# The norms of query and key moved from VectorE to GpSimd in a fused attention and feed-forward kernel, with a new merge order of its streams

## The reference

```
h = layernorm(x) * (1 + ca) + sa
x = x + ga * attention_A(h)       # 16 heads of 8; softmax over 512 keys of k.v * temperature, applied to q
h = layernorm(x) * (1 + cb) + sb
x = x + gb * F(h)                 # F is two layers, below
# one layer of F, 8 heads of 64:
  q, k, v = split(shift_token(x) @ wqkv)
  q = q / clip(norm(q), 1e-12) * q_scale ;  k = the same with k_scale    # one norm per token and head
  q, k = rotary_xpos(q, k)
  x = x + local_attention(q, k, v) @ wo      # windows of 64 tokens, each sees itself and the one before
  h = layernorm(shift_token(x)) * g + b
  x = x + (a * gelu(g')) @ w2 + b2           # a, g' = split(h @ w1 + b1)
```

## Time and profile before

| | |
|---|---|
| median of 3 runs | 1196.69 us (1193.58 to 1197.32) |
| the profiled execution, whole | 1196.15 us |
| its span, first to last instruction | 1194.3 us |
| busy of the span: PE, DVE, ACT, POOL | 997.0, 949.4, 918.2, 508.1 us |
| mean granted PE clock | 0.948 of full speed |

### The profile page before, as it was taken

One profiled execution on the slowest core, in us unless ns is written; L12 is line 12 of the kernel. 1 busy time (PEld: TensorE's weight loads), 2 busy tenths in 40 slices (PEclk: granted clock), 3 DMA queues, 4 the chain that ended last, 5 costly groups with the idle time before them and its releaser, 6 DMA issues. The chain is left out here.

```text
span 1194.3 us, 23996 instructions
## 1 busy us (share of the span) xinstructions
PE 997.0 (83%) x8124; PEld 510.0 (43%) x8124; DVE 949.4 (79%) x1947; ACT 918.2 (77%) x2782; POOL 508.1 (43%) x578
## 2 busy tenths in 40 slices
PE   2677787768888798778868897899999789999898
PEld 2232232223323352234336444655664357545664
DVE  4789898888869777986884699779769976789865
ACT  1698979899978988887659566868886587958983
POOL 5012143212105321343474058647823676348830
PEclk8699989999989898998989998999999999999999
DMA  5541305232204103001011001101110020001200
GB/s 206 180 142 36 106 1 146 62 107 71 72 0 130 43 28 115 10 10 24 1 31 34 10 1 32 33 1 32 33 41 10 10 63 16 18 1 32 46 20 27
DMA packets 28009, 59.18 MB, mean 50 GB/s; under 512 B 6192, under 2 KB 6384, under 8 KB 26736
## 3 DMA queue, kind: packets, MB, share of 16 engines
q1 hardware_dynamic: 27120, 56.33, 16.7%
q10 hardware_dynamic: 768, 1.31, 0.3%
HBM read 23.98 MB, written 18.87 MB: 36 GB/s over the span
## 5 line engine op out<-in xcount | busy, mean ns | idle before, releaser
L905 ACT ACTIVATE E<-psum,neg_max 128x512 f32<-128x512 f32 x512 | 346.6, 716 | 64.2 <-DVE neg_max L1191 45.9
L1191 DVE TENSOR_REDUCE neg_max<-psum 128x2 f32<-128x1024 f32 x256 | 307.5, 1214 | 58.7 <-PE psum L465 56.7
L465 PE MATMUL psum<-v_rows,k_rows 64*128 64x512 f32 x512 | 130.3, 514 | 106.0 <-ACT E L905 79.6
L998 ACT ACTIVATE rot_work<-psum,neg 128x128 f32<-128x128 f32 x512 | 184.3, 412 | 17.9 <-DVE neg L1284 11.0
L838 POOL TENSOR_TENSOR rot_work<-rot_work,rz 128x512 f32<-128x512 f32 x128 | 133.0, 1047 | 141.0 <-DVE rz L1289 140.9
L825 POOL TENSOR_TENSOR work<-work,rot_work 128x512 f32<-128x512 f32 x96 | 121.7, 1273 | 129.6 <-DVE rot_work L1262 129.3
L465 PEld LDWEIGHTS psum<-v_rows,k_rows 64*128 64x128 f32 x512 | 52.8, 196 | 250.6 <-ACT E L905 116.1
L803 POOL TENSOR_TENSOR qz<-qT,rz 128x32 f32<-128x32 f32 x128 | 30.8, 241 | 300.7 <-DVE rz L1195 299.8
L523 PE MATMUL psum<-wqkv_sb,hs 128*128 128x512 f32 x288 | 144.0, 622 | 6.8 <-DVE hs L1248 3.8
L474 PE MATMUL psum<-E,qz 128*32 128x512 f32 x1024 | 148.2, 653 | 0.2 <-POOL qz L803 0.2
L998 ACT ACTIVATION_READ_ACCUMULATOR rot_work<-psum,neg 128x1 f32 x512 | 126.7, 252 | 0.0
(11 more groups left out here) (140 smaller groups left out, 1784.7 us busy)
## 6 DMA issues: line engine op xcount, KB each, us to landing
k_rows<-k_scr SPq DMA_DIRECT2D x128, 64.0 KB, 1.9
work<-v_al SPq DMA_DIRECT2D x16, 512.0 KB, 4.4
v_rows<-v_scr SPq DMA_DIRECT2D x124, 64.0 KB, 1.9
work<-v_al SPq DMA_DIRECT2D x16, 384.0 KB, 5.7
k_scr<-hi SPq DMA_DIRECT2D x16, 256.0 KB, 3.0
k_scr<-lo SPq DMA_DIRECT2D x16, 256.0 KB, 3.3
v_scr<-hi SPq DMA_DIRECT2D x14, 256.0 KB, 2.9
v_scr<-lo SPq DMA_DIRECT2D x14, 256.0 KB, 3.1
```

Of the source, the lines that this page charges most:

```text
L465: pe.matmul(bank, k_rows[r:r + 64, half, hh, P * j:P * (j + 1)], v_rows[r:r + 64, b % 2, hh, :], start=True, stop=True).then_inc(full, 1)
L905: act.activation(E[:, (b * NG + g) % E_RING, 2 * half + m, :], pair[:, m], ACT.Exp, bias=neg_max[:, n, m:m + 1], accum_out=z[:, n, m:m + 1 ...
L998: last = act.activation(pr[s][:, u % PR_SLOTS, w, :], bank[:, 2 * W * w:2 * W * (w + 1)], ACT.Exp, bias=neg2[s][:, u, w:w + 1], accum_out= ...
L1191: dve.tensor_reduce(neg_max[:, n, :], pair, AX.X, ALU.max, negate=True).then_inc(max_ready, 1)
```

## The change

POOL now adds the upper 32 squares of each head to the lower 32, in place (`b_half`, a 128x256 add), and DVE sums 32 columns per head in a step of its own, `b_squares`, that waits for `sq_half`. The clamp, on POOL, is one `tensor_scalar` with two constants, and the `clamp` tensor and its fill go. The Newton step is on POOL in four dependent operations of 128x32; DVE's two steps of it, `b_norm` and `b_rnorm`, go. ACT's part is as it was. On POOL the order for each tile is `b_half`, then `b_rotary`; the norm of keys stands after the fourth tile, its Newton step after the fifth. `ORDER` and `BANKS` are new throughout; the steps per batch of F rise from 48 to 72 on POOL and from 87 to 95 on DVE, and stay 94 on PE and 88 on ACT.

```diff
+            def b_norm(s, k, l, w):
+                passed(pool, ss_ready[s], (k * L + l) * 2 * J + J * (2 - w))
+                v = ss[s][:, :, w, :]
+                pool.tensor_scalar(v, v, NORM_MIN2, SHIFT2, ALU.max, ALU.mult).then_inc(ss_all[s], 1)
+
+            def b_rnorm(s, k, l, w):
+                n = (k * L + l) * 2 + 1 - w
+                pool.wait_ge(ss_rsqrt[s], n + 1)
+                v, r, t = (a[s][:, :, w, :] for a in (ss, rn, nt))
+                pool.tensor_tensor(t, v, r, ALU.mult).then_inc(rn_chain[s], 1)
+                pool.wait_ge(rn_chain[s], 4 * n + 1)
+                pool.tensor_tensor(t, t, r, ALU.mult).then_inc(rn_chain[s], 1)
+                pool.wait_ge(rn_chain[s], 4 * n + 2)
+                pool.tensor_scalar(t, t, -0.5, 1.5, ALU.mult, ALU.add).then_inc(rn_chain[s], 1)
+                pool.wait_ge(rn_chain[s], 4 * n + 3)
+                pool.tensor_tensor(r, r, t, ALU.mult).then_inc(rn_chain[s], 1)
+
+            def b_half(s, k, l, n):
+                pool.wait_ge(sq_ready[s], (k * L + l) * 2 * J + n + 1)
+                v = sq[s][:, n % 2, :].rearrange("p (h a r) -> p h a r", h=H, a=2)
+                pool.tensor_tensor(v[:, :, 0], v[:, :, 0], v[:, :, 1], ALU.add).then_inc(sq_half[s], 1)
...
-                dve.tensor_reduce(ss[s][:, i, w, :], sq[s][:, n % 2, :].rearrange("p (h d) -> p h d", h=H),
+
+            def b_squares(s, k, l, n):
+                i, w = ROTATIONS[n]
+                dve.wait_ge(sq_half[s], (k * L + l) * 2 * J + n + 1)
+                dve.tensor_reduce(ss[s][:, i, w, :], sq[s][:, n % 2, :].rearrange("p (h d) -> p h d", h=H)[:, :, 0:32],
                                   AX.X, ALU.add).then_inc(ss_ready[s], 1)
-
-            def b_norm(s, k, l, w):
-                passed(dve, ss_ready[s], (k * L + l) * 2 * J + J * (2 - w))
-                v = ss[s][:, :, w, :]
-                dve.scalar_tensor_tensor(v, v, NORM_MIN2, clamp[:], ALU.max, ALU.mult).then_inc(ss_all[s], 1)
-
-            def b_rnorm(s, k, l, w):
-                dve.wait_ge(ss_rsqrt[s], (k * L + l) * 2 + 2 - w)
-                newton(ss[s][:, :, w, :], rn[s][:, :, w, :], nt[s][:, :, w, :], b_link_of(s, k)).then_inc(rn_ready[s], 1)
```

On PE, the `x` work done when the scores of A's batches 1 to 7 begin, and at A's end, is 0.0, 0.01, 0.22, 0.24, 0.39, 0.67, 1.0, 1.35 batches before and 0.0, 0.4, 0.76, 1.12, 1.37, 1.67, 2.1, 2.24 after. Before, the first `z` stands 109 letters behind the last `a` on PE, after 7 behind it; of PE's last 60 letters 31 are `z` after and 13 before. The first lines of POOL's string are:

```diff
-        "aaaaaaaaaaaaaaaaaaaaaaaaaaaaaaaaaaaaaaxaxaxaxxxaxxaxxxaaxaaaxxaxxaaaaaaaaaaaaaaaaaaaaaaaaaxxaxaaaaaa"
...
+        "aaaaaaaaaaaaaaaaaaaaaaxxxxxxxxxxxxxxxxxxxxxaaxxaxaxxxxaaaaxaxxxaxxxaxaaaaaaaaxxxxxaxxxaxxxaxaaxxxaxa"
```

More of the change, by code:

```diff
@@ new lines @@
+        "aaaaaaaaaaaaaaaaaaaaaaaaaaaaaaaaaaaaaaaaaaaaaaaaaaaaaaaaaaaaaaaxaxxxxxxxxxxaaaaaxxaaaxxxxaaaaaaaaaax"
+        "xaxxaaaaxxaaxxaxaxxxxaxaxxaaaxxxaaaaxaaaxaaaaaxaaaaxaxxxxxxaxaaaaxxxxxaaaxxxaaxaxaaaaaaaaaaxxaaxxaxa"
+        "axaaaaaaaxaaxxxaxaaaxxaaaxaaaxxxaaaaaxxxxaxaaxaxxaaaxaxaaaaaaaxaaaaaaxaaxxxxaaxaxxaaaxaaaaaaxaaaaaxx"
+        "xxxaxaxxaaxxaaaaaaaaaxxaaaaaaxxaaxxaaaaaaaaaaaaaaaaxxxxaaaxxaaxaaxaaaaaaxxxaaxxaxxxaaaxxaaxaaaxaaaax"
+        "aaaaaaaxaaaaaaaxaxxxaaxxaxaaxaaaaxaxxxxxxxxxaaaaaaaaaxaxxxxaxaaaaaaaaaxaxxxaaxxaaxaxxxxaaaxxxxaxaaax"
@@ new lines @@
+        "xaxaaxaxaaaaxaaaaaaaaxxxaxaxxaaaxxaaaaxaaaaaaaxaaxxxxxxaaaxxaaaxxaaaaaaxaaxaxxxxaaaaaaaaaaaaaaaxxxxa"
+        "aaaaaaaaaaaaaaaaaaaaaxaxaxxxxxyzxxxxzyyyyyyyyyyzzzzzzzzzxxxxxxzzxzzzyyzxxyyyyxxxxxxyxyxyyxyyzxxxzxyy"
+        "xzxzyyyzxyyyyzzyyyzyzzyzyzzzyzxxzxxxxyzzyyzyyyyzyzyyzyyyyyyyxxxxzyxzzzzzzyyxxyyyyzxxxzxxzxzzzxxxzzzz"
+        "zyyxxxyyxyxyzzxyyyzzyyzxyzyxxxxyyyxxxyyzxzzyzyzzyxzzzzyxxzxxzxxxxxxyzyyyyyzzzxxyyxxyzzxxzzzyxxxxzyyx"
+        "xyyyyyyyyxxxzxzxxzzzzxxyyzyxyyxyzxxxzxxyyyyzxyyzzzzxzzzzzxzxxyyxxxyyxyyyzzzzzzyyyxxxxxyyxyxyxxyzxzyz"
@@ new lines @@
+        "xyyxyyyyyzxyyxyyzzyxxyyzyyzyzzyyzzzxyzzzxxyyzzxyzzzyzxxxzxyyyzyyzzyzyyyyzyyyyxxyyxxzyzzyxxxxyyzzyxxx"
+        "xxzxzxzzxxxzxxzzyzxzyzyzyxxyyyzxyzyyxyyyzzyyzxyyyxxyxyxxzyxzzzzyzzyzxzyzxxzzzxxyxxxxxzzxxyyzzxzyzxyx"
+        "yxxzyzyzzyxzyxxzxxyyxxxyyyyxxyyxxxyyzzxyxyzxxxyyxzyxzzxzxxyxzyyxyyyyzzyzzzzzzzxzxzyxyzxxyyyyyzzzyzyy"
+        "xxyxyxxxxyxxyyyzxxzzyzzzzxxzzzxzzzxxyyyzzyyzzzzyyyzyyzyyyyzyzyzxxzyxyxxyxxxyyzzzzzxxxxxzzzyzzzzzzyyz"
+        "zyyxxxxyyzyxxzxyyzzxzxxyyxyyyxzyyyzzyzxxxzzzxzzzxzzzzyzzzyzzyyzyzyzzzyyzyyyzzzzz"
@@ L104 @@
[L104 to L108, removed]
+        "aaaaaaaaaaaaaaaaaaaaaaaaaaaaaaaaaaaaaaaaaaaaaxxaxaaxxxxxxxxxxxaaaaxxaxaxxaxxaaaaxxaxxaaaxxaxxxxaxxax"
@@ L122 @@
 BANKS = (
[L123 to L133, removed]
+    "0123424024024023502350135023550224602640240240240240264603606360631436023501502350245604624024045246"
+    "1014603046301350130135013501045630013506236032501634016351356154302460240245140204254025035012402246"
+    "0520461201460264023403252014526056406240245024651236056360131351345150123501305244204626410520420626"
+    "4024062325302513051340624023502350260246406134530506240652605406131402450143125350245012305204454202"
+    "4540134036145403013061351300451203156024602402646012603105351024130501345602402402402345024024024024"
+    "0240201073435743257326376723242324276733707605047466707327067007601270276405127523262040261242616745"
+    "7412060123602347521021302307076012726121731703721035012057145010357150127105712610510310370767234263"
+    "2170413501675370760170170130123570213457354676505473247237043701203172701273014601435263420474265270"
+    "4072136746047654507657601376512063712507362701354150742041703575160560514017016024076306146253465301"
+    "0341370320120301072017013702746036071246372457432574673674767026406762401612746376746017350413634526"
+    "136756072360426706040765676765075070701701700"
 )
@@ L273, in build @@
         s_silexp, s_sil, s_setup = sem("s_silexp"), sem("s_sil"), sem("s_setup")
-        s_gcol, s_tables, s_clamp, s_qz, s_kzero = (
-            sem(n) for n in ("s_gcol", "s_tables", "s_clamp", "s_qz", "s_kzero"))
+        s_gcol, s_tables, s_qz, s_kzero = (
+            sem(n) for n in ("s_gcol", "s_tables", "s_qz", "s_kzero"))
         s_chain = sem("s_chain")
@@ L847, in b_stream @@
                                 enter_wait(pool, s, k)
+                            b_half(s, k, l, n)
+                            yield
                             b_rotary(s, k, l, n)
                             yield
+                            if n == J - 1:
+                                b_norm(s, k, l, 1)
+                                yield
+                            if n == J:
+                                b_rnorm(s, k, l, 1)
+                                yield
                             for i in {J: (0,), J + 1: range(1, J)}.get(n, ()):
@@ L852, in b_stream @@
                                 yield
+                        b_norm(s, k, l, 0)
+                        yield
+                        b_rnorm(s, k, l, 0)
+                        yield
                         for i in range(J):
```

84 lines of the change are left out of this document (32 added, 52 removed).

## The result

The changed kernel takes 1187.27 us (median of 5, 1183.78 to 1189.60) against 1196.33 before: a ratio of 0.9923 [0.9907, 0.994], 9 us faster where 39 were forecast. The direction was right, the size four times too large. The time lies outside the forecast's own range (1135 to 1180) and inside the wide one (1120 to 1194), near that one's upper edge.

A forecast was written before the change was run, and what follows sets the result against it. PE was taken to bound the steady stretch, with DVE, ACT and PE taking turns in A's part. 93.0 to first gating, 535.5, 0.7 and 526 give span 1155, plus 1.9: 1157 us; own range 1135 to 1180, wide 1120 to 1194.

The forecast's parts named there:

- The reading of the bound: No engine is full over the span; PE limits the steady stretch from 650 to 1150 us, busy 92%.
- The durations: Sum of squares 405 ns, half add 724, small GpSimd operations near 241; VectorE loses about 92 us, GpSimd rises to about 639.
- the price of `x` beside A: A batch of `x` work costs 65 us beside A, against 95.5 in the last part.
- A's part: Seven batches of A with 0.32 batch of `x` beside each, at 76.5 us: 535.5 us.
- Can shorten it: In A's part, VectorE's relief of 3.7 us a batch can shorten the batch.
- The last part: After A, 5.75 batches of F at 90.9 us, plus 3 us for a thinner tail: 526 us.
- I cost them at nothing: GpSimd's slack covers 16 half adds a batch (11.6 us), so they cost nothing.
- Equal; nothing: The norm's chain on GpSimd, about 1.5 us against 1.8 us before, counts as no change.
- R1: POOL limits the last part: 97 us a batch, total 1192 us; chance 0.14.
- R2: A is held by POOL's queue, 84 us per A batch, total 1210 us; chance 0.14.
- R3: Packing gets better: A batch 73.5 us, batch of F 88, total 1119 us; chance 0.13.
- R4: Order moves work and gains nothing: `x` beside A costs 95.5 us per batch, total 1195 us; chance 0.05.

The follow-up runs named there:

- e2: Changed kernel with clamp, Newton step and 64-column sums back on VectorE, no half adds; only order and banks differ from the kernel before: 1209.0 us, ratio 1.0107.
- e13: Norms on GpSimd, no half adds, 64-column sums on VectorE; a second rearrangement of neighbouring order letters, starting from e8: 1162.4 us, ratio 0.9725.
- e4: Changed kernel with only the half adds undone, VectorE summing 64 columns a head: 1186.8 us, ratio 0.9908.
- e3: Changed kernel without half adds, VectorE still summing only the lower 32 columns of each head, upper half left out: 1174.6 us, ratio 0.9831.
- e7: e2 with neighbouring order letters of different streams swapped, operations all on VectorE: 1172.3 us, ratio 0.9793.
- e8: e4 (norms on GpSimd, no half adds, 64-column sums) with neighbouring order letters swapped: 1166.8 us, ratio 0.9761.
- e14: All norms on VectorE, a second rearrangement of neighbouring order letters, starting from e7: 1173.8 us, ratio 0.9807.
- e9: Kernel before, its operations and placing of `x` kept, neighbouring order letters swapped: 1222.0 us, ratio 1.0217.
- e10: Changed kernel with A's row maximum taken over only the first 256 of each bank's 512 columns: 1161.4 us, ratio 0.9724.
- e5: Changed kernel with only clamp and Newton step back on VectorE, half adds kept on GpSimd: 1212.4 us, ratio 1.0120.

## Why the prediction was wrong, step by step

**The reading of the bound** held: PE's work stayed 997.0 us in the changed kernel, and its whole gain was PE's idle time. (In the experiments PE's busy time went from 983 to 1018 us with the granted clock, which the forecast had no term for.)

**The durations** held within 2% for the two large operations (410 for 405 ns, 731 for 724), and GpSimd came to 634 us for 639. VectorE did not: it fell by 57 us, not by 91. The removed 143.7 and the added 52.4 us are as forecast; of the 34 missing, 25 stand in the groups of seven other operations with all operands in SBUF, five of them the layer norm's. The other 9 are about the overlap of durations: 128 operations fewer at 0.08 us each, by the figure for VectorE given above, are 10 us (an estimate). The one that grew most, the same line before and after (durations min/median/max):

```profile
L1149 DVE TENSOR_TENSOR tmp<-tmp,rstd x32: 161/162/165, 11.4 to 1176.0; 128x4 f32<-128x4 f32 x32
```

```profile
L1183 DVE TENSOR_TENSOR tmp<-tmp,rstd x32: 161/163/1202, 11.4 to 1164.6; 128x4 f32<-128x4 f32 x32
```

What stretches it the timeline of the changed kernel shows (start, duration):

```profile
786.96 1.28 POOL L825 TENSOR_TENSOR work<-work,rot_work 128x512 f32<-128x512 f32 x1
787.05 1.20 DVE L1183 TENSOR_TENSOR tmp<-tmp,rstd 128x4 f32<-128x4 f32 x1
788.18 0.74 POOL L848 TENSOR_TENSOR rot_work<-rot_work 128x256 f32<-128x256 f32 x1
788.29 0.65 DVE L1184 SCALAR_TENSOR_TENSOR rstd<-tmp,rstd 128x4 f32<-128x4 f32 x1
```

Each ends within 0.02 us of the GpSimd operation that had begun before it: 787.05 + 1.20 = 788.25 against 786.96 + 1.28 = 788.24. The Trainium skill (SBUF — State Buffer, Who interferes with whom) says that a VectorE operation with two SBUF inputs contends with a GpSimd operation that reads SBUF. The trace agrees for these two pairs. The prediction had put it at 1 to 2 us. Four of the seven groups, 11.5 of the 25 us, have one tile as input, which that sentence does not speak of. One of them was seen held in the same way: the copy `var<-stats` of 128x4 (171 ns at the median) that began at 756.68 us took 1.02, to within 0.03 us of the end of the GpSimd multiplication that began at 756.64 and took 1.03. A fuller GpSimd alone does not explain it: the group of L1183 takes 5.2 us in the kernel before and 11.1 in e2, both with GpSimd at 506 to 508 us, 12.3 in the changed kernel, and 5.2 again in e13, with GpSimd at 547. The order decides which two meet. PE waits behind the layer norm: it stood 11.1 us, 8 times, for L1188 before L593, against 2.4 us at the same place before.

**The step that failed is the price of `x` beside A**: 65 us per batch of F, against 95.5 in the last part, and "That is the gain". The prediction divides 88.7 us by 1.36 batches counted in letters. By PE's work (A's part and the start, less eight batches of A: 374.35 + 53.96 - 329.8 = 98.5 us, at 83.4 each) they were 1.18. A step of `x` near the cut is shorter than the mean step, so letters overstate the work. And the 54.1 us of the bare batch already hold 13.0 us of PE's idle time, which every batch of A has, with `x` or without: the same rows say that 374.35 - 7 x 41.1 = 86.6 us of PE's work were bought with 88.7 us. Set beside the last part's 1.11 us per microsecond of PE, that is a gain of a tenth and not of a third. The marginal price in the runs is 1.04 in the changed kernel and 1.13 in e2, where no operation changed: between nothing and a fifteenth. Per batch of `x` by letters the changed kernel paid 82.5/0.89 = 93 us, not 65.

**A's part**, 535.5 us forecast, was 549.9: 78.6 us a batch, not 76.5. It is 545 to 571 us in all eleven kernels that lay 2.2 batches beside A and kept the full maximum, whatever was done to VectorE and GpSimd. "Can shorten it" (DVE's relief) was right for 9 to 11 us (e4 to e3, e2 to changed), of at most 7 x 3.7 = 26.

**The last part**, 526 us forecast, was 539.6. The steady stretch was even better than assumed (PE 92.8% from 700 to 1150). Missed were the size, 488.9 us of PE's work = 5.86 batches, not 5.75 (10 us), and the two ends: 56.4 us for 45.7 of PE at the start of `y` and `z`, 33.2 for 25.5 at the end, together 13 us over the steady rate where the forecast has 3. That the term itself can be had, e7, e8, e13 and e14 show, with 523 to 525.

**"I cost them at nothing"**, of the half adds, failed: e3 prices them at 12.7 us. Their cover, GpSimd's idle time, was there (46% of the span), but it lay in front of other instructions: 18.3 us of VectorE's waits and 31.7 of GpSimd's stood at the half adds themselves, since a queue's idle time covers an instruction only if its inputs have come when its turn comes. "Equal; nothing" for the norm chain was wrong to the other side: leaving VectorE's queue went with 5 to 22 us.

**The rivals.** R1 did not happen: POOL was busy 343 of 450 us (76%) in the steady stretch and PE was fuller than before. R2 did not either, though its place showed: the first batch of A with `x` took 97.6 us, 0.4 batch of `x` ran in it, and PE waited 2.2 us for `qz` in the whole A part. R3 did not: A's batches took 78.6 us, not 73.5, and PE was at 93% in the steady stretch, not 95%. R4 (95.5 us per batch at the margin, chance 0.05) had the right mechanism, which the forecast's own rows could have told: it put A's part at 552 us (549.9 measured), the last part at 547 (539.6) and the total at 1195. That the time lies inside the wide range is luck: its upper edge was put there for R1, which did not happen.

## What to carry to other kernels

The price of work beside other work is read as span per microsecond of the full engine's work, in both places, never per step of a list; here it was 0.99 to 1.13 beside A and 1.11 after it, so that moving a batch by itself gained little or nothing. Whether placing and fitted order together gain more is open (e9 failed to show it). An order written out by hand belongs to the operations it was made for: test a change of operations only with an order fitted to each side, and hold two orders for each before believing a difference under 10 us. An addition that stands between two engines costs its wait even where its own engine idles. And before a difference of medians is put down to waits, look whether the full engine's busy time for the same work has moved with its clock.

## What was not expected of the hardware

A VectorE operation on 128x4 takes 162 ns, and took up to 1202 ns beside a GpSimd operation, to the end of which it was held in the pairs looked at; the groups in which this was seen grew by some 25 us, and other orders of the same work lost less. The halved sums of squares, with one input from SBUF, kept to 351 to 422 ns. In A's part PE's granted clock was 0.93 before and in the changed kernel, 0.96 in e10 and 0.90 in e5: the same matmuls took 453.4 us of PE in the changed kernel, 441.8 and 471.9 in the other two. PE idled 96.5, 84.4 and 99.4 us there; over all kernels its idle time and its clock do not go together, and the cause is open.
